# Sparse attention steps: the next rows' transposition, the rotation sum and the index weights' bias moved

## The reference, cut to what matters

```python
qkv = x @ w_qkv.T + b_qkv
Q, K = (_rope(Q), _rope(K))
iq = (x @ w_iq.T + b_iq).reshape(B, S, IDX_HEADS, IDX_DIM)    # 4 heads of 64
ik = x @ w_ik.T + b_ik
iw = x @ w_iw.T + b_iw                                        # 4 weights a row
head_scores = relu(einsum('bqhd,bkd->bhqk', iq, ik))
index_scores = einsum('bhqk,bqh->bqk', head_scores, iw)
# logits of the 32 keys with the highest index scores, softmax, times V, times w_o
```

## Time and profile before

| what | value |
|---|---|
| median of 3 runs | 567.16 us (565.54 to 567.82) |
| time of the profiled execution | 566.95 us |
| its span | 565.1 us |
| PE / DVE / ACT / POOL busy | 80% / 67% / 60% / 51% of the span |
| granted TensorE clock, mean | 0.922 |

### The profile page before, as it was taken

The page is one execution under the profiler, slowest core; times in us unless marked ns, Lnnn a source line. Parts: engine busy times, 40 slices in busy tenths (PEclk is TensorE's granted clock), DMA queues, the critical chain, the costliest instruction groups (busy, mean ns, idle before and its releaser), DMA issues. The chain is left out here.

```text
span 565.1 us, 11633 instructions
## 1 busy us (share of the span) xinstructions
PE 451.0 (80%) x3048; PEld 390.7 (69%) x3048; DVE 380.0 (67%) x1501; ACT 337.2 (60%) x934; POOL 288.4 (51%) x329
## 2 busy tenths in 40 slices
PE   1789985859999986999889998889647668786991
PEld 1578865859999874676666766667437568676981
DVE  5789976425666622999999999999957234434661
ACT  1568852226776616889999899998521245434650
POOL 5753440454430025987778777775410633665442
PEclk9989995979999989999999999999756969888996
DMA  8942232131331110011111111110111321121110
GB/s 224 288 135 77 74 90 25 44 88 53 99 87 35 34 34 15 9 37 32 28 30 30 42 44 28 30 30 21 36 35 5 84 57 48 56 64 56 39 36 17
DMA packets 45070, 32.42 MB, mean 57 GB/s; under 512 B 13524, under 2 KB 39508, under 8 KB 45012
## 3 DMA queue, kind: packets, MB, share of 16 engines
q1 hardware_dynamic: 39892, 19.11, 12.2%
q0 software_dynamic: 5120, 12.62, 8.5%
HBM read 19.10 MB, written 12.62 MB: 56 GB/s over the span
## 5 line engine op out<-in xcount | busy, mean ns | idle before, releaser
L629 PE MATMUL bank<-X,w 128*128 x624 | 91.0, 292 | 18.3 <-ACT X L834 16.3
L639 PE MATMUL bank<-WE,hT 128*128 x624 | 89.2, 289 | 14.3 <-ACT hT L847 6.8
L427 POOL DMA_INDIRECT big<-rows,gidx x64 | 61.5, 961 | 74.7 <-DVE gidx L1147 28.2
L629 PEld LDWEIGHTS bank<-X,w 128*128 128x128 f32 x624 | 82.0, 205 | 22.3 <-issue 21.9
L639 PEld LDWEIGHTS bank<-WE,hT 128*128 128x128 f32 x624 | 81.3, 203 | 17.0 <-issue 16.9
L834 ACT ACTIVATE X<-bank 128x128 f32<-128x128 f32 x64 | 17.9, 280 | 94.6 <-PE bank L620 60.9
L1179 DVE TENSOR_SCALAR hT<-bank,w 128x128 f32<-128x128 f32 x156 | 47.6, 346 | 39.0 <-issue 12.2
L660 PE MATMUL bank<-xbT,WB 128*128 128x256 f32 x224 | 59.2, 394 | 13.2 <-ACT xbT L872 8.5
L839 ACT ACTIVATE w<-WE 128x644 f32 x78 | 57.5, 738 | 3.1 <-DVE big L1191 2.8
L847 ACT ACTIVATE hT<-bank,w 128x128 f32<-128x128 f32 x156 | 48.7, 367 | 13.4 <-PE bank L629 10.1
L447 POOL DMA_INDIRECT X<-x,pidx x32 | 31.7, 989 | 48.7 <-DMA x<-big 41.2
(11 more groups left out here) (161 smaller groups left out, 1026.6 us busy)
## 6 DMA issues: line engine op xcount, KB each, us to landing
WE<-w_experts SPq DMA_DIRECT2D x2, 2048.0 KB, 11.5
rows<-xf SPq DMA_DIRECT2D x32, 128.0 KB, 2.2
rows<-X SPq DMA_DIRECT2D x32, 128.0 KB, 2.7
X<-x SPq DMA_DIRECT2D x4, 512.0 KB, 7.6
x<-big SPq DMA_DIRECT2D x32, 64.0 KB, 1.5
big<-rows,gidx POOLq DMA_INDIRECT x64
WB<-w_idx SPq DMA_DIRECT2D x1, 640.0 KB, 5.7
WE<-b SPq DMA_DIRECT2D x1, 512.0 KB, 12.9
```

Of the source, the lines that this page charges most:

```text
L427: pool.indirect_dma_start(xg[:, j, :], None, rows_dram[n], bass.IndirectOffsetOnAxis(ap=gidx[:, j:j + 1], axis=0)).then_inc(f["g"][j % G_R ...
L629: mm = pe.matmul(bank[r + 2 * (k // 2)][:, k % 2 * P:(k % 2 + 1) * P], w1[st.slot(1, 4)][:, k * P:(k + 1) * P], moving, start=True, stop=True)
L639: mm = pe.matmul(bank[4 + r][:, 0:D], hT[r][:, k, :], WE[:, bass.ds(expert[(s - 2) % TURN], 1), W2_AT + k * D:W2_AT + (k + 1) * D].rearran ...
```

## The change

The transposes of item s+1 move from the head of step s+1 to the place behind the value product of step s, in front of `index_scores(0)`, and write bank 4; those of item 0 stand ahead of the loop. On ACT `normalise_b` moves in front of the write of `vb`, and `turned` from the second half to the end of the first. `add_heads(0)` moves behind the rotation sum on POOL. `rowc` and the one-row product go; DVE adds the bias in `index_weights`, behind the second round. `opens` is false for steps behind T.

```diff
-        rowc = sb("rowc", [1, C * IDX_HEADS])
+        biw_bc = sb("biw_bc", [P, IDX_HEADS])
-            return (st.base - HEAD) % TURN == 0 or st.base == lag or st.base == T
+            return st.base <= T and ((st.base - HEAD) % TURN == 0 or st.base == lag or st.base == T)
-            for c in range(C):
-                sp.dma_start(rowc[:, c * IDX_HEADS:(c + 1) * IDX_HEADS], b_iw).then_inc(ld_w, 16)
+            sp.dma_start(biw_bc[:, :], b_iw.rearrange("a e -> (a e)").partition_broadcast(P)).then_inc(ld_w, 16)
...
# POOL
-                    add_heads(b, r, 0)
                     pool.wait_ge(b_["rp"], 2 * (b + 1))
                     after(pool, b_["S"], C * (b - 1))
                     pool.tensor_tensor(qr[r][:, :, :], qk[r][:, 0:2, :], qk[r][:, 2:4, :], ALU.add).then_inc(b_["qr"], 1)
+                    add_heads(b, r, 0)
                     add_heads(b, r, 1)
...
# PE
+            def turn_rows(b, r):
+
+                pe.wait_ge(b_["xb"], b + 1)
+                for c in range(C):
+                    mm = pe.transpose(bank[4][:, c * P:(c + 1) * P], xb[r][:, c, :], ident)
+                mm.then_inc(b_["T"], 1)
+
+            turn_rows(0, 0)
             for st in (Step(s) for s in range(B + 4)):
...
-                if st.on(0, B):
-                    b, r = st.item(0), st.slot(0, 2)
-                    pe.wait_ge(b_["xb"], b + 1)
-                    after(pe, b_["iwe"], b)
-                    after(pe, tails[1]["xfT"], b - 3)
-                    for c in range(C):
-                        mm = pe.transpose(bank[5][:, c * P:(c + 1) * P], xb[r][:, c, :], ident)
-                    mm.then_inc(b_["T"], 1)
...
-                    pe.matmul(bank[5][:, S:S + C * IDX_HEADS], ones[0:1, :], rowc[:, 0:C * IDX_HEADS], start=True, stop=False)
+                    after(pe, tails[1]["xfT"], b - 3)
                     for c in range(C):
                         mm = pe.matmul(bank[5][:, S + c * IDX_HEADS:S + (c + 1) * IDX_HEADS], xbT[r][:, c * P:(c + 1) * P],
-                                       WB[:, 9 * D:9 * D + IDX_HEADS], start=False, stop=(c == C - 1))
+                                       WB[:, 9 * D:9 * D + IDX_HEADS], start=True, stop=True)
                     mm.then_inc(b_["pj"], 1)
...
+                if st.on(-1, B):
+                    turn_rows(st.item(-1), st.slot(-1, 2))
                 if st.on(0, B):
                     index_scores(0)
...
# ACT
-                    projected(3)
-                    act.wait_ge(b_["pj"], 5 * (b + 1))
-                    after(act, b_["wk"], C * (b - 1))
-                    act.activation(iw[r][:, :, :],
-                                   bank[5][:, S:S + C * IDX_HEADS].rearrange("p (c h) -> p c h", c=C),
-                                   ACT.Copy).then_inc(b_["iwe"], 1)
+                    projected(3, (0,))
                 if st.on(-1, B):
                     normalise_b(st, -1)
+                if st.on(0, B):
+                    projected(3, (1,))
...
# DVE
+            def index_weights(b, r):
+
+                dve.wait_ge(b_["pj"], 5 * (b + 1))
+                dve.tensor_tensor(iw[r][:, :, :], bank[5][:, S:S + C * IDX_HEADS].rearrange("p (c h) -> p c h", c=C),
+                                  biw_bc[:, :].unsqueeze(1).to_broadcast([P, C, IDX_HEADS]), ALU.add).then_inc(b_["iwe"], 1)
...
                 def beside(i):
 
+                    if i == 1 and st.on(0, B):
+                        index_weights(st.item(0), st.slot(0, 2))
```

More of the change, by code:

```diff
@@ L406, in _ @@
                     b, r = st.item(1), st.slot(1, 2)
-                    pool.wait_ge(ld_w, 80)
+                    pool.wait_ge(ld_w, 64)
                     pool.wait_ge(a_pt, b + 1)
@@ L547, in _ @@
                 if st.base == 6:
-                    pe.wait_ge(ld_w, 80)
+                    pe.wait_ge(ld_w, 64)
                 if st.on(6, B):
@@ L871, in turned @@
                 after(act, b_["idx"], 2 * C * (b - 1))
-                act.activation(xbT[r][:, :], bank[5][:, 0:S], ACT.Copy).then_inc(b_["xbT"], 1)
+                act.activation(xbT[r][:, :], bank[4][:, 0:S], ACT.Copy).then_inc(b_["xbT"], 1)
             normalise_b(Step(0), 0)
@@ L877, in _, with projected @@
                 b, r = st.item(0), st.slot(0, 2)
-                def projected(pair):
+                def projected(pair, which=(0, 1)):
                     act.wait_ge(b_["pj"], 5 * b + pair + 1)
-                    for i in (2 * pair, 2 * pair + 1):
+                    for i in (2 * pair + w for w in which):
                         src = bank[2 + pair % 2][:, i % 2 * S:(i % 2 + 1) * S]
@@ L928, in _ @@
                                            bank[i][:, :].rearrange("p (h k) -> p h k", h=2), ACT.Relu).then_inc(b_["rel"], 1)
-                    if c == C - 1 and st.on(-1, B):
-                        turned(st.item(-1), st.slot(-1, 2))
                     if st.on(0, B):
@@ L936, in _ @@
                         ins.then_inc(b_["prt"], 1)
+                    if c == 0 and st.on(-1, B):
+                        turned(st.item(-1), st.slot(-1, 2))
                     if c == 0 and st.on(3, B):
```

## The result

| | before | after |
|---|---|---|
| median | 566.35 us (565.2 to 567.82, 4 runs) | 572.93 us (571.54 to 575.24, 4 runs) |
| profiled execution, span | 566.95, 565.1 us | 572.45, 570.6 us |

The account below looks back on a forecast made before the run. The prediction took the chain through PE (`prT`, value product, scores, `rel`) to set the pace, with ACT level in the middle steps. 566.95 + 4.4 + 1.5 - 3.1 = 569.75 us, rounded to 569.8; range 566.2 to 572.7.

Parts of the forecast that it names:

- The bound: Sparse attention's middle steps: the chain `prT`, value product, scores, `rel` on PE sets the pace; lengthening it costs in full.
- Rival 1: Middle steps: ACT sets the pace, so its freed time is won, 0.88 us a step; 552.5 us, chance 0.12.
- Rival 2: Middle steps and start: transposes cost only PE's bare issue, 0.2 us, the start one delay; 567.3 us, chance 0.13.
- rival 3: Ends of the expert stages give nothing; 572.7 us, or 571.2 if one end pays; chance 0.13.
- The middle: Steps 2 to 14: transposes in front of the scores make them 0.34 us later in 13 steps, +4.4 us.
- My upper bound, 0.45: Middle steps: the scores' delay per step if the transpose pair costs its whole 0.44 us.
- Steps 0 and 1: Start of sparse attention: scores wait for `xb`, +0.86 us in step 0; loss at step 1's `pen` +1.5 us.
- The ends: Last tile of both expert stages: dropping DVE's load of eight registers gives twice -1.55, -3.1 us.
- DVE and POOL: Sparse attention steps: `qr` moved earlier frees 0.55 us of DVE, which becomes waiting for `pen`; no time won.

Follow-up runs that it names:

- e4: Changed kernel with the next rows' transposes moved from in front of the first index scores to behind them; ratio 0.9971 to the kernel before.
- e5: Changed kernel with the two transposes of the next rows made twice, four in all; ratio 1.0179 to the kernel before.
- e6: Kernel before with ACT's part of the change alone, `xb` ahead of `vb`; ratio 1.0003 to the kernel before.
- e7: Kernel before with POOL's part alone, `qr` (the rotation sum) ahead of both head sums; ratio 0.9996 to the kernel before.
- e1: Kernel before without the register load in front of the last tile of both expert stages; ratio 0.9961 to the kernel before.
- e11: Kernel before without those last register loads and with 92 instead of 60 transposes in the block ahead of the sparse attention; ratio 0.9941 to it.
- e2: Changed kernel with the register load in front of the last tiles put back; ratio 1.0174 to the kernel before.
- e3: Changed kernel with 92 instead of 60 transposes in the block ahead of the sparse attention; ratio 1.0112 to the kernel before.
- e9: As e8, with the second half of the probabilities turned ahead of the last pair of projections; ratio 0.9737 to the kernel before.
- e8: Changed kernel, first scores before value product, second behind transposes, `xfT` behind second `rel`, `mask_logits` awaiting both halves, 92-transpose block; ratio 0.9843 to the kernel before.

## Why the prediction was wrong

**The bound, right.** The chain through PE set the pace, and who lengthens it pays in full: e4, e5, e6 and e7 show it from four sides. Rival 1 (ACT sets the pace, 552.5 us) is out, since e6 frees 0.69 us of ACT and wins nothing. Rival 2 (bare issue, 0.2) is out by the step, rival 3 by e1, e11 and e2.

**The middle, +4.4, measured +5.7: a size was off.** The transposes start 1.13 us behind the value product (291.61 to 292.74), as worked out. The failed piece is "Transposes that had to wait let the next product start 238.98 - 238.70 = 0.28 later": the scores came 0.37 behind. I had taken the row from transposes in front of projections. The trace of the kernel before has a nearer row, the transposes of `xf` in front of the second scores, and they cost 0.31:

```profile
291.19 0.38 PE L522 MATMUL bank<-cst,xf 128*128 128x128 f32 x2
...
291.50 1.17 PE L679 MATMUL bank<-ik,iq 64*128 64x256 f32 x8
```

That pair costs 0.31 in the changed kernel too, so the product that follows explains 0.03 of the missing 0.09, and the other 0.06 stay open. In all it is 0.43 us for the scores instead of 0.34, and 0.45 for the step. My upper bound, 0.45, hits the size by luck and not by its reason: it took the whole duration of the pair, 0.44, and the pair cost 0.37.

**Steps 0 and 1, +1.5, measured +3.3: the step that failed.** "I put the loss at step 1's `pen` at +1.5 us, an estimate between 0.8 (one step's delay) and 1.7 (both)." The first scores come 8.11 us behind the first transposes instead of 5.77, +2.34: 1.43 of it are the slow passes, and the rest, 0.9, is the +0.86 that I had worked out. From the scores of step 0 to those of step 1 it is 10.38 instead of 9.40, +0.98, where I had hoped that most would be won back; `xb` of step 1 waits 0.37 us for `nb`. From the scores of step 1 to its `pen` nothing is lost. So the order costs 1.9, a little above my bound, and the clock 1.4, of which I had no term. I had counted that "all that is behind moves with it", and had not asked what an earlier end of the block does to the idle time behind it.

**The ends, -3.1, measured -3.2: right.** The first stage gave 1.46, the second 1.74 (554.60 - 553.02 is 1.58 an end, which I had rounded down to 1.55). The Trainium skill (Runtime: NRT & Kernel Launch, Instruction fetch mechanics) would have made it an estimated 2.7 by its 200 ns a register; the rows of 1.82 and 1.84 us were the better guide. **DVE and POOL, 0: right.** `add_third` fell to 0.45 and 0.48, `index_weights` took 0.17 and was never held. The rule of the Trainium skill (SBUF — State Buffer, Who interferes with whom) on DVE instructions with two SBUF inputs fits the stretch: 1.03 us beside POOL's `qr`, 0.45 without.

The sum of what was measured is -1.46 + 3.33 + 5.69 - 0.38 - 1.74 = +5.4, against +5.5 of the profiled executions. Of the 2.7 us that I missed, 1.3 lie in the middle and 1.8 at the start; the stretch in front of the second expert stage gave 0.4 that I had not looked for, and its cause is open.

## What to carry to other kernels

Write down the loop that sets the pace as a chain of instructions, and cost each thing that is put into it, also if it is small and prepares work early, by a row of the timeline in which the same kinds of instruction follow each other; what is saved beside the chain becomes waiting. The place counts more than the work: the same two transposes cost 0.4 us a step in front of the scores and next to nothing behind them, and putting the scores first in that chain won about 1 to 2% beside what the loads gave. When an engine's work ends earlier, look what stands idle behind it, and at the clock of what comes next.

## What was not expected of the hardware

PE's clock. After a block of transposes, idle time of 3.95 to 4.84 us was followed by 14 passes in 5.1 to 5.5 us (after the change, granted clock 0.78 and 0.79 in the windows from 212 to 220 us), and idle time of 0.47 to 2.65 us by the same passes in 3.6. No length between these was run. A longer block cured it in the old order (passes of 3.62 us in e11, 5.15 in e1), and not in the changed one: in e3 PE waited 0.98 and 0.74 us in the steps behind, and the clock fell after that (0.69 from 212 to 216 us). That those waits made it fall is not shown.

A DVE instruction can be held over two of POOL's. The Trainium skill (SBUF — State Buffer, Who interferes with whom) says that the shared port is an exclusive lock; here an `nb` of 0.15 us and an `xf` of 0.34 were held for 2.85 and 3.11 us, from before the first multiplication of POOL to the end of the second. Both had started 0.34 and 0.53 us before POOL's multiplication, while POOL was still issuing a gather, and in e9 an `nb` that started 0.35 before the multiplication, with the same gather still going, was not held. What decides is open. In e8 this one event cost 7.0 us, since the clock fell behind it.
